# First attention layer of a gated four-layer stack: a quad of heads worked on in two halves

## The reference, cut to what matters

```python
x = x + tanh(g_xattn[0]) * _L0_xattn_ref(_layernorm(x), ctx, ...)   # the layer that the change is in
x = x + tanh(g_ffn[0])   * _L0_ffn_ref(_layernorm(x), ...)
x = x + tanh(g_xattn[1]) * _L1_xattn_ref(_layernorm(x), ctx, ...)
x = x + tanh(g_ffn[1])   * _L1_ffn_ref(_layernorm(x), ...)

def _L0_xattn_ref(x_query, x_context, Wq, Wkv, Wp, bp, ln_g, ln_b):
    q = layernorm(heads(x_query @ Wq), ln_g, ln_b) * 4        # 16 heads of 16
    k = layernorm(heads(x_context @ Wkv[:, :256]), ln_g, ln_b)
    v = heads(x_context @ Wkv[:, 256:])
    attn = softmax(einsum('bhqd,bhkd->bhqk', q, k))           # 112 x 375 for each head
    return einsum('bhqk,bhkd->bhqd', attn, v) @ Wp + bp
```

## Time and profile before

| | us |
|---|---|
| median of 3 runs | 630.76 (627.73 to 632.69) |
| the profiled execution | 631.75 |
| its span in the trace | 629.9 |
| what lies around the span | 1.85 |

### The profile page before, as it was taken

One profiled execution on the slowest core, in us unless ns is written; L12 is line 12 of the kernel. 1 busy time (PEld: TensorE's weight loads), 2 busy tenths in 40 slices (PEclk: granted clock), 3 DMA queues, 4 the chain that ended last, 5 costly groups with the idle time before them and its releaser, 6 DMA issues.

```text
span 629.9 us, 13692 instructions
## 1 busy us (share of the span) xinstructions
PE 586.4 (93%) x5588; PEld 491.0 (78%) x5588; DVE 398.0 (63%) x809; ACT 308.6 (49%) x590; POOL 283.1 (45%) x240
## 2 busy tenths in 40 slices
PE   7789989999988999999999999988779999999994
PEld 6657667767655787878788887866679999998994
DVE  7563675686676545566656666668717677755761
ACT  2234545545554455455545545556206666545541
POOL 5955385577560037446465464550110443221224
PEclk9979999999999999999999999998989999999998
DMA  7900190000000000000000000028053756645212
GB/s 254 350 6 1 42 404 30 2 1 2 3 1 2 2 1 1 8 2 23 2 22 16 9 16 9 23 83 334 16 165 125 239 208 200 202 134 181 67 24 24
DMA packets 24171, 50.93 MB, mean 81 GB/s; under 512 B 7408, under 2 KB 16928, under 8 KB 20768
## 3 DMA queue, kind: packets, MB, share of 16 engines
q1 hardware_dynamic: 18784, 45.33, 19.7%
q0 software_dynamic: 4224, 3.70, 3.3%
q10 hardware_dynamic: 1088, 0.88, 0.5%
HBM read 37.89 MB, written 13.31 MB: 81 GB/s over the span
## 4 chain that ended last, share of the span: by engine, by line
PE 71%; POOL 13%; DVE 10%; ACT 2%; issue 2%; DMA 1%; SPq 0%; POOLq 0%; DVEq 0%; ACTq 0%
PE ps L58 12%; PE ps L59 11%; PE ps L60 11%; POOL sr L1622 10%; PE ps L701 5%; PE ps L667 4%; PE ps L683 4%; DVE KN L1019 4%; PE ps L633 2%; PE ps L542 2%; PE ps L743 2%; PE ps L647 2%; PE ps L623 2%; PE ps L561 2%; PE ps L577 1%
## 5 line engine op out<-in xcount | busy, mean ns | idle before, releaser
L1664 POOL TENSOR_SCALAR P<-P,rinv 112x487 f32<-112x487 f32 x56 | 85.7, 1542 | 63.1 <-DVE rinv L1052 62.9
L1622 POOL TENSOR_TENSOR sr<-sv,mhalf 125x32 f32<-125x32 f32 x16 | 87.0, 5438 | 1.3
L58 PE MATMUL ps<-XGf,WH 128*128 128x256 f32 x256 | 73.2, 286 | 1.4 <-DVE XGf L1237 1.4
L374 POOL DMA_INDIRECT out<-WS,rows_i x16 | 28.4, 1773 | 101.1 <-ACT WS L1524 97.1
L1019 DVE TENSOR_REDUCE KN<-ps 112x4 f32<-112x1500 f32 x32 | 55.0, 1719 | 29.0 <-PE ps L542 28.9
L59 PE MATMUL ps<-XGf,WH 128*128 128x256 f32 x256 | 73.2, 286 | 0.0
L60 PE MATMUL ps<-XGf,WL 128*128 128x256 f32 x256 | 73.2, 286 | 0.0
L1308 DVE TENSOR_TENSOR WL<-WR,WH 128x1024 fp32r<-128x1024 f32 x48 | 57.5, 1223 | 12.1 <-ACT WH L1576 9.5
L1450 ACT ACTIVATE P<-ps,nm 112x487 f32<-112x487 f32 x64 | 42.1, 663 | 45.9 <-DVE nm L1044 44.4
L1401 ACT ACTIVATE P<-ps 125x1344 f32<-125x1344 f32 x32 | 41.3, 1292 | 43.5 <-PE ps L561 43.4
L58 PEld LDWEIGHTS ps<-XGf,WH 128*128 128x128 f32 x256 | 49.9, 195 | 1.7 <-DVE XGf L1237 1.7
(11 more groups left out here) (235 smaller groups left out, 1535.6 us busy)
## 6 DMA issues: line engine op xcount, KB each, us to landing
WR<-in_gupT SPq DMA_DIRECT2D x16, 1024.0 KB, 7.1
WR<-in_dwnT SPq DMA_DIRECT2D x8, 1024.0 KB, 10.6
xs<-ZT SPq DMA_DIRECT2D x14, 516.0 KB, 5.7
P<-xs SPq DMA_DIRECT2D x24, 128.0 KB, 8.9
CT<-in_ctxT SPq DMA_DIRECT2D x1, 2250.0 KB, 10.2
Wk<-in_L_xattn_Wk SPq DMA_DIRECT2D x2, 512.0 KB, 12.0
Wv<-in_L_xattn_Wv SPq DMA_DIRECT2D x2, 512.0 KB, 12.6
out<-X SPq DMA_DIRECT2D x8, 112.0 KB, 1.9
```

Of the source, the lines that this page charges most:

```text
L58: e.matmul(out, ah, bh, start=start, stop=False)
L1622: e.tensor_tensor(sr[:, p, :], sv[:, p, :], mhalf[0:125, 0:32], ALU.pow).then_inc(s("sr"), 1)
L1664: e.tensor_scalar(P[:, k, 0:487], P[:, k, 0:487], rinv[:, k:k + 1], None, ALU.mult).then_inc(s("psc"), 1)
```

## The change

**Halves.** `S0`, `max0`, `st` and `ex` get a second index z. Half z covers heads 2z and 2z + 1 of the quad, their two groups of 32 rows and the two banks 2z and 2z + 1. `qt2`, `qt2c` and `V0` stay whole. The semaphores `sc0`, `smax`, `st` and `ex` now count halves, and all waits on them are scaled. A half of `S0` waits for the same half of `ex` two quads before, a half of `st` of quad q for the same half of `max0` of q + 1; `qt2` and `V0` wait for both halves.

**Order.** `QUAD` places the halves: half 1 of `S0` 2.7 after half 0, half 1 of `st` 2.95 after half 0. In the resulting list `S0` of (q, 1) stands right before `st` of (q - 1, 0), and `S0` of (q, 0) right before `st` of (q - 2, 1); in one of a batch's eight such places a value product (`v`) stands between the two. The other tables get new times, most of them moved by under 2; `T1` becomes 5.5 * 32 + 6. No other computation is added or taken away.

```diff
-QUAD = ((-0.75, "S0"), (0.52, "max0"), (3.51, "qt2"), (3.89, "qt2c"), (7.55, "st"), (8.59, "ex"), (10.69, "V0"))
+QUAD = ((-0.75, "S0", 0), (0.48, "max0", 0), (1.95, "S0", 1), (2.7, "max0", 1), (4.35, "qt2"), (4.1, "qt2c"),
+        (7.5, "st", 0), (8.6, "ex", 0), (10.45, "st", 1), (11.36, "ex", 1), (12.6, "V0"))
...
-PREP = ((-37.87, "cs"), (-35.37, "norm", 0), (-32.44, "kp", 1, 0), (-32.74, "xt", 0), (-30.56, "xtc", 0),
+PREP = ((-40.0, "cs"), (-36.26, "norm", 0), (-32.44, "kp", 1, 0), (-32.74, "xt", 0), (-30.56, "xtc", 0),
...
-VALUES = ((-14.52, "v", 1, 0), (-13.63, "vc", 1), (-0.32, "v", 0, 0), (2.34, "v", 0, 1), (6.34, "vc", 0))
+VALUES = ((-14.52, "v", 1, 0), (-13.8, "vc", 1), (-2.47, "v", 0, 0), (3.18, "v", 0, 1), (6.46, "vc", 0))
...
-PAIR = ((0.31, "S"), (3.2, "sc"), (9.69, "T"), (13.33, "V"))
+PAIR = ((0.31, "S"), (2.77, "sc"), (9.69, "T"), (13.33, "V"))
...
-    T1 = TQ * NQUAD + 4
+    T1 = TQ * NQUAD + 6
...
                 elif stage == "S0":
-                    q, = i
+                    q, z = i
                     b, k = divmod(q, 4)
                     if q >= 2:
-                        w.wait_ge(s("ex"), q - 1)
+                        w.wait_ge(s("ex"), 2 * (q - 2) + z + 1)
...
-                    for g in range(4):
+                    for g in (2 * z, 2 * z + 1):
...
-                    w.wait_ge(s("smax"), min(q + 2, NQUAD))
+                    w.wait_ge(s("smax"), min(2 * (q + 1) + z + 1, 2 * NQUAD))
...
-                    for j, g in itertools.product(range(3), range(4)):
+                    for j, g in itertools.product(range(3), (2 * z, 2 * z + 1)):
...
                 elif stage == "max0":
...
-                    w.wait_ge(s("sc0"), q + 1)
-                    e.tensor_reduce(heads(KN[b % 2][0:NQ, 3, :])[:, 4 * k:4 * k + 4, 16], ps[0:NQ, 0:4, 0:NC], AX.X,
+                    h = 4 * k + 2 * z
+                    w.wait_ge(s("sc0"), 2 * q + z + 1)
+                    e.tensor_reduce(heads(KN[b % 2][0:NQ, 3, :])[:, h:h + 2, 16], ps[0:NQ, 2 * z:2 * z + 2, 0:NC], AX.X,
                                     ALU.max, negate=True).then_inc(s("smax"), 1)
...
                 elif stage == "ex":
...
-                    e.activation(PQ[:, q % 3, :].rearrange("p (g n) -> p g n", g=4), ps[0:125, 0:4, 0:3 * NQ],
-                                 ACT.Exp).then_inc(s("ex"), 1)
+                    cs = slice(6 * z * NQ, 6 * (z + 1) * NQ)
+                    e.activation(PQ[:, q % 3, cs].rearrange("p (g n) -> p g n", g=2),
+                                 ps[0:125, 2 * z:2 * z + 2, 0:3 * NQ], ACT.Exp).then_inc(s("ex"), 1)
```

More of the change, by code:

```diff
@@ L100 @@
-         (-6.2, "kq", 1, 1), (-2.2, "kss", 1, 1), (-0.5, "norm", 1, 0), (1.36, "xt", 1, 0), (1.3, "xtc", 1, 0),
-         (1.2, "kp", 1, 0, 0), (3.8, "kp", 1, 0, 1), (4.9, "kq", 1, 0), (6.4, "kss", 1, 0), (4.4, "ksc", 1, 1),
-         (6.5, "spk", 1, 0), (6.86, "spkc", 1, 0), (9.2, "spk", 1, 1), (9.8, "spkc", 1, 1), (11.76, "ksc", 1, 0),
[1 row of a table added]
+         (-10.25, "ksc", 0, 1), (-9.18, "spk", 0, 0), (-7.7, "spkc", 0, 0), (-8.13, "spk", 0, 1),
+         (-6.61, "spkc", 0, 1), (-3.5, "ksc", 0, 0), (-5.69, "qaff", 0), (-2.7, "spk", 0, 2), (-2, "spkc", 0, 2),
@@ L103 @@
+         (-1.2, "spq", 0), (-0.8, "spqc", 0), (-3.88, "rs0", 1), (-8, "kp", 1, 1, 0), (-7.21, "kp", 1, 1, 1),
+         (-6.41, "kq", 1, 1), (-2.2, "kss", 1, 1), (-0.5, "norm", 1, 0), (1.36, "xt", 1, 0), (1.3, "xtc", 1, 0),
+         (0.95, "kp", 1, 0, 0), (3.8, "kp", 1, 0, 1), (4.9, "kq", 1, 0), (6.4, "kss", 1, 0), (4.4, "ksc", 1, 1),
+         (8.39, "spk", 1, 0), (6.86, "spkc", 1, 0), (9.2, "spk", 1, 1), (9.8, "spkc", 1, 1), (12.57, "ksc", 1, 0),
          (13, "qaff", 1), (14.6, "spk", 1, 2), (15.2, "spkc", 1, 2), (17.5, "spq", 1), (18.1, "spqc", 1))
-PREP = ((-37.87, "cs"), (-35.37, "norm", 0), (-32.44, "kp", 1, 0), (-32.74, "xt", 0), (-30.56, "xtc", 0),
-        (-29.47, "kp", 1, 1), (-28.27, "kq", 1), (-26.72, "kss", 1), (-26.6, "kp", 0, 0), (-23.9, "kp", 0, 1),
+PREP = ((-40.0, "cs"), (-36.26, "norm", 0), (-32.44, "kp", 1, 0), (-32.74, "xt", 0), (-30.56, "xtc", 0),
+        (-29.98, "kp", 1, 1), (-29.04, "kq", 1), (-26.72, "kss", 1), (-26.6, "kp", 0, 0), (-23.9, "kp", 0, 1),
@@ L114 @@
+        (-5.95, "spk", 2), (-4.0, "spkc", 2))
+VALUES = ((-14.52, "v", 1, 0), (-13.8, "vc", 1), (-2.47, "v", 0, 0), (3.18, "v", 0, 1), (6.46, "vc", 0))
+TAIL0 = ((28.92, "ob"), (31.1, "obT"), (30.86, "aw"), (33.27, "awT"), (33.66, "aT"), (43.91, "wo"),
+         (46.33, "res", 1), (47.8, "stats", 1), (52.03, "norm", 1), (72.8, "xt", 1), (72.61, "xtc", 1), (75.4, "f2"),
+         (77.43, "res", 2), (77.59, "rtanh"), (79, "radd"), (79.6, "stats", 2), (82.32, "norm", 2), (85.21, "xt", 2),
          (84.68, "xtc", 2))
-PAIR = ((0.31, "S"), (3.2, "sc"), (9.69, "T"), (13.33, "V"))
@@ L118 @@
-PAIR_LAST = ((-1.33, "S"), (4.41, "T"), (9.45, "V"))
-FIRST1 = ((-18, "cs1"), (-13.5, "k1", 0), (-11.6, "k1c", 0), (-11.5, "k1", 1), (-9.6, "k1c", 1), (-9.5, "k1", 2),
+PAIR = ((0.31, "S"), (2.77, "sc"), (9.69, "T"), (13.33, "V"))
+PAIR_LAST = ((-1.33, "S"), (4.41, "T"), (9.47, "V"))
+FIRST1 = ((-21.91, "cs1"), (-13.5, "k1", 0), (-11.6, "k1c", 0), (-11.0, "k1", 1), (-9.6, "k1c", 1), (-9.5, "k1", 2),
           (-7.6, "k1c", 2), (-7.5, "k1", 3), (-5.31, "k1c", 3), (-5.1, "q1"), (-3.6, "q1c"), (-3.5, "v1", 0),
-          (-1.6, "v1c", 0), (-1.5, "v1", 1), (-0.77, "v1c", 1), (-0.67, "v1", 2), (1.23, "v1c", 2), (7.6, "v1", 3),
+          (-1.6, "v1c", 0), (-1.5, "v1", 1), (-0.77, "v1c", 1), (-0.67, "v1", 2), (0.7, "v1c", 2), (7.6, "v1", 3),
@@ L128 @@
          (27.27, "v1c", 3))
-TAIL1 = ((12.96, "aT"), (14.41, "wo"), (16.12, "res", 3), (18.96, "stats", 3), (20.63, "norm", 3), (22.55, "xt", 3),
-         (23.31, "xtc", 3), (23.07, "rt0"), (23.91, "rt1"), (26.62, "rt2"), (28.05, "rt3"), (32.49, "rt4"),
+TAIL1 = ((12.96, "aT"), (14.41, "wo"), (15.72, "res", 3), (18.58, "stats", 3), (20.63, "norm", 3), (22.56, "xt", 3),
+         (23.31, "xtc", 3), (24.7, "rt0"), (23.91, "rt1"), (26.62, "rt2"), (27.75, "rt3"), (32.49, "rt4"),
          (33.31, "rt5"))
-TAIL_LAST = ((1.58, "rv"), (4.84, "rb"), (6.92, "rbc"), (8.1, "aT"), (9.72, "wo"), (10.67, "res", 3),
+TAIL_LAST = ((1.58, "rv"), (5.67, "rb"), (6.92, "rbc"), (8.1, "aT"), (9.72, "wo"), (10.67, "res", 3),
@@ L163, in attention_order @@
     for q in range(NQUAD):
-        for d, stage in QUAD:
-            at(TQ * q + d, stage, q)
+        for d, stage, *i in QUAD:
+            at(TQ * q + d, stage, q, *i)
     pair_at = [T1 + TP * p if p < NPAIR - 4 else T1 + TP * (NPAIR - 4) + TL * (p - NPAIR + 4) for p in range(NPAIR)]
@@ L432, in first_layer_left @@
         def first_layer_left(w, b):
-            w.wait_ge(s("st"), 4 * (NB - 1 + b))
+            w.wait_ge(s("st"), 8 * (NB - 1 + b))
             w.wait_ge(s("av0"), 4 * (NB - 1 + b))
@@ L548, in tensor_attention @@
                     bk = take(stage, q)
-                    w.wait_ge(s("smax"), q + 1)
+                    w.wait_ge(s("smax"), 2 * q + 2)
                     e.transpose(ps[:, bk, 0:NQ], KN[b % 2][0:NQ, 3, k * 128:(k + 1) * 128],
@@ L567, in tensor_attention @@
                     b, k = divmod(q, 4)
-                    w.wait_ge(s("ex"), q + 1)
+                    w.wait_ge(s("ex"), 2 * q + 2)
                     if k == 0:
@@ L657, in tensor_attention @@
                     if p == 0:
-                        w.wait_ge(s("smax"), NQUAD)
-                        w.wait_ge(s("ex"), NQUAD)
+                        w.wait_ge(s("smax"), 2 * NQUAD)
+                        w.wait_ge(s("ex"), 2 * NQUAD)
                     else:
@@ L1128, in keys_copy @@
             if b >= 2:
-                w.wait_ge(s("sc0"), 4 * (b - 1))
-                w.wait_ge(s("st"), 4 * (b - 1))
+                w.wait_ge(s("sc0"), 8 * (b - 1))
+                w.wait_ge(s("st"), 8 * (b - 1))
             dst = KT[b % 2][:, :, j * 125:(j + 1) * 125]
@@ L1761, in sync_attention @@
             w.wait_ge(s("dve0"), ZT_SET)
-            w.wait_ge(s("sc0"), 8)
+            w.wait_ge(s("sc0"), 16)
             dz = xs.rearrange("(p r) d -> p (r d)", p=128)
```

23 lines of the change are left out of this document (8 added, 15 removed), and 2 rows, old and new, of the table FIRST.

## The result

| | before | changed |
|---|---|---|
| median of 20 runs each, us | 631.17 (627.53 to 633.18) | 633.75 (632.05 to 636.6) |
| ratio, 95% interval | | 1.0050 [1.0036, 1.0064] |
| span of the profiled execution, us | 629.9 | 634.6 |

What follows compares the result with a forecast made beforehand. The prediction took TensorE, busy 93% of the span, as the bound. Gaining 13.5 us against 9.3 us more work gave -4.2 us: 627.5 us profiled, 627.0 us as plain median, 0.6% faster, range 622 to 633.

Steps and rivals of the forecast that it cites:

- TensorE bounds the layer, and a shorter chain can win no more than its gaps: First layer: TensorE busy 93% of the span; its gaps, 15.15 us, limit the gain unless it gets less to do.
- Maximum and Exp of a half, 932 and 733 ns: Half-size maxima on VectorE and exponentials on ScalarE: 4.6 and 5.6 us more in all, inside those engines' idle time.
- The waits in the turn, 8.0 us, go: Banks 0 to 3: a half's turn takes 3.7 us instead of 5.07, so TensorE's waits for maxima and exponentials vanish.
- A pair takes 0.88 us, a half alone 0.83: TensorE: half S0 and half st run side by side, 2.6 us more in all; an unpaired half costs a whole's time.
- in order: Rival, chance 0.15: half st starts only behind the half S0's last start, a pair takes 1.26 us, kernel 647 us.
- TensorE has 9.3 us more to do: TensorE's added work in the first layer: 2.6 us for pairs, 5.8 for unpaired halves, 0.9 at the layer's end.
- the 2.0 us of tails hidden in the waits: Each of 20 waits hides 0.1 us of the preceding matmul, counted busy in the trace; 2.0 us counted as gained.
- A broken place: In seven batches a value product stands between the halves, so a half S0 runs alone: 0.83 us each, 5.8 us.
- 13.5 us gained, 11.5 of them in gaps: TensorE's gain: 8.0 us of turn waits, 2.0 of hidden matmul tails, 3.5 of waits behind VectorE's copies.
- Waits added: TensorE's queue: no wait new in kind, only finer; 0.8 us left between S0 and st; cost taken 0.
- The rest of the order costs nothing, `T1` within 3 us: Other stages' new times, mostly moved under 2, T1 by 2: cost taken 0, with 3 us on either side.
- The end of the layer, 0.9 us: The last three halves of st lack partners, taking about two blocks of 0.85 us instead of one: 0.9 us.

Runs made afterwards that it cites:

- run 3: The kernel of run 2 with the last quad's two st halves directly behind each other; 631.13 us, 1.0007 to the kernel before.
- run 2: Changed kernel with the value product moved behind the half st, only in batches 2 to 7; 632.05 us, 1.0011 to the kernel before.
- runs 5 and 6: Against the kernel before: halves with old times but T1 + 6, 645.4 us, 1.0238; whole quads with all new times, 637.32 us, 1.0113.
- Runs 11 to 13: last_st_paired with V0 and qt2, V0 alone, or qt2 alone behind the next pair; 1.0278, 1.0208 and 1.0102 to the kernel before.
- last_st_paired: Kernel of run 3: changed kernel, value product behind the half st from batch 2, last two st halves together; 631.13 us, 1.0007.
- run 1: Changed kernel with each batch's value product put behind the half st instead of between the halves; 633.72 us, 1.0049 to the kernel before.

## Why the prediction was wrong, point by point

- **TensorE bounds the layer, and a shorter chain can win no more than its gaps:** right. Price and gain both went through TensorE's gaps, 14.65 and 8.75 us.
- **Maximum and Exp of a half, 932 and 733 ns:** right, 938 and 735. What more they take of VectorE and ScalarE lies beside TensorE's work.
- **The waits in the turn, 8.0 us, go:** right, none is left in the list of waits for `st` and `S0` but one of 0.7 us for a copy.
- **A pair takes 0.88 us, a half alone 0.83:** right, 0.85 and 0.82 to 0.84. The rival "in order" falls: the half `st` starts 0.01 us after the half `S0`, not 0.41. The Trainium skill's page "TensorE: Matmul & The Clock Gate" (Part 3, Packing small matmuls) says that matmuls keep program order. Record by record this trace differs: six records of `st` start before the second records of the `S0` ahead of it (147.50 to 147.89), in other groups of rows. As order between the first records of whole calls the rule stands against nothing here, and the 1.15 us of run 3 are what it would give; order in their ends can't be read, since the records don't name their call.
- **TensorE has 9.3 us more to do:** too small. The trace shows 9.8, but the two don't compare as they stand. The forecast put the 2.0 us of tails hidden in the waits among the gains, and the trace counts them as busy; so its terms mean 7.3 us more of busy time and 11.5 less of gaps. Busy time was missed by 2.5 us. Of these, 1.6 are the second half of the first quad's `S0`, alone in the stretch of half clock (33.54 us in the trace), which the sum left out. A broken place costs 0.75 us of TensorE where 0.83 was reckoned, but the kernel's time pays for only three of the six that run 2 mended.
- **13.5 us gained, 11.5 of them in gaps:** this is the term that failed. The gaps fell by 5.9. The old waits went as forecast: 12.0 us of the 12.6 that the earlier trace rows name, where 11.5 were reckoned. The step that failed is "Waits added. None is new in kind; they are finer ... Cost taken: 0". A half quad of delay was put into the turn, and `qt2`, `V0` and the stages that take their banks in rotation were left with less slack: they need both halves, and the second half of maximum and Exp now stands later. In the list, `qt2` stood 2.99 behind the maximum and now stands 1.65 behind its second half; `V0` stood 2.10 behind Exp and now stands 1.24 behind; that the halves are shorter gives back only 0.78 and 0.56 us of it. 7.0 us of new waits came, measured in front of `qt2`, `V0` and `xt`, and runs 5 and 6 show that those of `V0` and `qt2` come with the halves. That it is the slack is argued from the list, not tested by itself. I had checked the room between `S0` and `st`, the two stages that became halves, and not that of the stages that stay whole. Runs 11 to 13 show that this slack isn't to be had by placing `qt2` and `V0` behind the next pair: something behind them is due too.
- **The rest of the order costs nothing, `T1` within 3 us:** wrong for whole quads (4.5 us by `T1` alone, 1.1% with all new times), about right for the halves (1 us at most). With `T1` at 6, the halves change the ratio from 1.0113 to 1.0050 under the new times, and from 1.0052 to 1.0238 under the old ones. So the parts of this change have no prices of their own; what one costs hangs on the other. The forecast added them.
- **The end of the layer, 0.9 us:** too small. 2.75 us were lost from batch 7's first `S0` on. The pair of run 3 gives back 0.7 of them by the traces, `T1 + 4` with its edits another 0.7 in this stretch; the rest stays open.
- **The sum:** 9.8 - 5.9 = +3.9 us instead of 7.3 - 11.5 = -4.2 in the first layer's window. 2.6 us more in the medians. What I named as a sign that the forecast is wrong, a middle batch over 23 us, is what the profile shows.

No version that I tried beats the kernel before: the best, last_st_paired, equals it (1.0007). At equal clock it is about 1 us behind (632.4 against 631.1 to 631.4 at 0.980, by the same lines). What stays open is why TensorE's clock falls in one place and not in another: the profiles show it at half for 3 to 21 us at the start of the layer or, in some, for 3 to 10 us near its end, and a profile is one execution.

## What to carry to other kernels

When a buffer's turn is cut into halves to break a ring, list every stage that still needs both halves, and reckon its slack with the second half's later end; a part of the wait taken from the ring, here 7.0 us for 12.0, comes back in front of such stages. Price the halves by the engine's time as well as by the waits: here four heads' products in separate groups of rows took 0.83 us and two heads' took 0.82, so a half costs as much as a whole unless its neighbour in the queue uses the other groups. Count a saving of the busy engine batch by batch: where the batch has other gaps, as in three of the six of run 2, it becomes gap. And on a kernel whose stages stand in a hand-set list, a change of structure and a change of order can't be priced apart.

## What was not expected of the hardware

- Two different kinds of fp32 product in separate groups of rows run side by side to the full: 4 records of 375 columns and 12 of 112 columns in 0.85 us together, each alone in 0.82 and 0.84 us. Two halves of `st`, six products each, took 1.15 us in the one place of last_st_paired where they stand together.
- The stretch of half clock at the layer's start was 7 us longer when TensorE had one more wait of about 1 us near 38.8 us (run 1), and batch 0 took 2.7 us more. The profiles are of one execution each, but the clocks of all runs (0.979 against 0.984) point the same way; that the wait is the cause isn't shown.
- The mean clock differs from run to run of one kernel by about 0.02, and 0.01 of it goes with 3 to 5 us, as much as most of the differences here.
